# Splitting eight weight chunks on GpSimd and summing four constant rows on VectorE in a two-layer fusion kernel

## The reference, cut to what matters

```python
h = tokenise(x)                      # 16 images, 37 tokens each, width 256
h = concat([h, txt], axis=1)         # 165 tokens per batch item
h = h + scan_attention(layernorm(h))
# layer 0 FFN: 8 experts in 4 groups, each token uses one group (2 experts)
gate = silu(einsum('td,edf->tef', xf, gate_w)); up = einsum('td,edf->tef', xf, up_w)
h = h + einsum('te,tef,efd->td', w, gate * up, down_w)
h = h + rope_attention(layernorm(h))
# layer 1 FFN: 4 experts, top 2
c     = gelu(b1) @ w2 + b2           # one row of 256 per expert
c_sum = c.sum(axis=0)
out   = gates . (y_sel - c_sel + c_sum)
```

## Time and profile before

| | us |
|---|---|
| median of 3 runs | 774.32 (773.2 to 774.41) |
| the profiled execution, its own time | 773.09 |
| its span in the profile | 771.3 |
| TensorE busy | 709.3 (92%) |
| VectorE / ScalarE / GpSimd busy | 453.9 / 370.8 / 292.4 |

### The profile page before, as it was taken

The page is one execution under the profiler, slowest core; times in us unless marked ns, Lnnn a source line. Parts: engine busy times, 40 slices in busy tenths (PEclk is TensorE's granted clock), DMA queues, the critical chain, the costliest instruction groups (busy, mean ns, idle before and its releaser), DMA issues.

```text
span 771.3 us, 18144 instructions
## 1 busy us (share of the span) xinstructions
PE 709.3 (92%) x6029; PEld 619.9 (80%) x6030; DVE 453.9 (59%) x1225; ACT 370.8 (48%) x871; POOL 292.4 (38%) x259
## 2 busy tenths in 40 slices
PE   5989974999999999988899998799999999999981
PEld 5769964889888897667789986688888888888871
DVE  5897677344444443437798988745454555455540
ACT  5898744433344433333667655343434343344430
POOL 2348101222333224114445430235556655564431
PEclk9999996999999999999999999899999999999996
DMA  9897998114122112127741279112233232323235
GB/s 265 190 212 86 140 163 267 42 29 120 28 41 41 27 22 35 22 61 199 152 56 18 39 92 303 47 36 43 43 53 55 42 47 48 55 45 45 36 36 155
DMA packets 42214, 66.22 MB, mean 86 GB/s; under 512 B 3680, under 2 KB 29264, under 8 KB 41616
## 3 DMA queue, kind: packets, MB, share of 16 engines
q0 software_dynamic: 22304, 39.19, 33.2%
q1 hardware_dynamic: 19664, 25.93, 10.6%
q10 hardware_dynamic: 192, 0.38, 0.1%
HBM read 65.80 MB, written 23.35 MB: 116 GB/s over the span
## 4 chain that ended last, share of the span: by engine, by line
PE 72%; DVE 15%; ACT 4%; DMA 4%; issue 2%; POOL 1%; POOLq 0%; SPq 0%; DVEq 0%
PE PS L1145 16%; PE PS L1158 15%; PE PS L852 14%; PE PS L889 8%; PE PS L867 3%; PE PS L2455 3%; PE PS L1513 2%; PE PS L2469 2%; ACT Y L2175 2%; PE PS L1130 1%; PE PS L1540 1%; DMA xs<-Y 1%; DMA X<-in_w_dram 1%; POOL X L1767 1%; DMA ccols<-in_cols_dram 1%
## 5 line engine op out<-in xcount | busy, mean ns | idle before, releaser
L1158 PE MATMUL PS<-X 128*128 x720 | 125.8, 273 | 1.9 <-ACT X L1227 1.9
L1324 POOL DMA_INDIRECT sum<-X,dest x45 | 89.4, 1986 | 96.3 <-ACT X L1227 79.3
L1145 PE MATMUL PS<-X 128*128 128x256 f16 (+1 forms) x768 | 122.7, 265 | 0.6 <-issue 0.6
L1217 ACT ACTIVATE X<-PS,X 128x256 f32<-128x256 f32 (+1 forms) x192 | 72.8, 462 | 103.2 <-PE PS L1145 103.2
L852 PE MATMUL PS<-Y,X 128*128 128x256 f16 x960 | 108.1, 273 | 0.5 <-DVE Y L1021 0.5
L852 PEld LDWEIGHTS PS<-Y,X 128*128 x960 | 93.8, 98 | 11.5 <-issue 0.7
L1145 PE MATMUL PS<-X,Y 128*128 128x256 f16 (+1 forms) x384 | 100.2, 264 | 0.0
L1158 PE MATMUL PS<-Y,X 128*128 x360 | 98.2, 273 | 0.0
L1116 POOL DMA_INDIRECT sum<-Y,dest x24 | 38.1, 1588 | 111.9 <-DVE Y L1049 108.3
L1145 PEld LDWEIGHTS PS<-X 128*128 x768 | 71.8, 97 | 10.3 <-issue 1.1
L1158 PEld LDWEIGHTS PS<-X 128*128 128x128 f16 x720 | 70.4, 98 | 10.8 <-issue 2.9
(11 more groups left out here) (408 smaller groups left out, 1390.2 us busy)
## 6 DMA issues: line engine op xcount, KB each, us to landing
X<-in_w_dram POOLq DMA_DIRECT2D x10, 1024.0 KB, 16.1
X<-in_w_dram POOLq DMA_DIRECT2D x8, 768.0 KB, 16.6
sum<-h SPq DMA_DIRECT2D x2, 2048.0 KB, 16.2
Y<-in_w_dram POOLq DMA_DIRECT2D x4, 1024.0 KB, 11.8
xs<-Y SPq DMA_DIRECT2D x2, 1040.0 KB, 6.5
xs<-Y SPq DMA_DIRECT2D x2, 1032.0 KB, 10.4
h<-in_txt_dram SPq DMA_DIRECT2D x2, 1024.0 KB, 16.9
Y<-in_patches_dram SPq DMA_DIRECT2D x3, 672.0 KB, 7.8
```

The costliest lines, as they stand in the source:

```text
L1145: ins = nc.tensor.matmul(PS[:, 2 * s + c // 2, (c % 2) * T1:(c % 2) * T1 + tokens], part[:, off:off + P], x_[:, slot, k, 0:tokens], start= ...
L1158: ins = nc.tensor.matmul(PS[:, 4 + a, 0:D], h_[:, s, c, a * P:(a + 1) * P], part[:, off:off + D], start=(s == 0 and c == 0 and n == 0), st ...
L1217: ins = nc.scalar.activation(hh1[:, s, c, 0:tokens], PS[:, 2 * s + c // 2, (c % 2) * T1:(c % 2) * T1 + tokens], ACT.Gelu, bias=bias1[:, sl ...
L1324: nc.gpsimd.indirect_dma_start(out=sum1, out_offset=bass.IndirectOffsetOnAxis(ap=dest[:, i:i + 1], axis=0), in_=y1buf[:, u % 2, i - first_ ...
```

## The change

In layer 0 the chunks 0 to 7 are no longer transferred with a cast and an addition. SyncE loads each as f32 into one of two buffers (`stage`, 128 x 1024 f32 each), the first two at once behind its other first loads, chunk n once chunk n - 2 is split. GpSimd copies a chunk to its high half as f16 and subtracts that from the buffer into the low half. The transfers carry the other 16 chunks: four casts and four additions of four chunks. The first addition is issued behind the split of chunk 6, the other three behind that of chunk 7. ScalarE negates 16 chunks in place of 18.

In layer 1 `biases_sum` is gone with its 96 matmuls. ScalarE copies `csum`, now the sum of the `b2` rows alone, and `rest1` ahead of `act_rows`. VectorE sums the four rows and `csum` with three additions and then subtracts, ahead of `dve_experts1`; the subtraction L1290 is gone from the first unit. TensorE waits for `rows_known` before `keep_clock(85, 3)`, and has three new fillers: `keep_clock(40, 3)` behind `pe_slots`, `keep_clock(45, 3)` ahead of the experts, and `keep_clock(18, 3)` where `meanwhile` stood.

```diff
-W0C, CAST, ADDED = XW0 // CW, 4, 3
-BY_ACT = range(6, W0C)
-NEGATED = (0, 2, 2, 2, 2, 2, 2, 2, 2, 2, 0)
+W0C, CAST, ADDED = XW0 // CW, 4, 4
+BY_ACT = range(8, W0C)
+NEGATED = (0, 2, 2, 2, 2, 2, 2, 2, 2, 0, 0)
...
-            pe.wait_ge(w0_added, 16 * W0C // ADDED)
+            pe.wait_ge(own_split, BY_ACT[0])
+            pe.wait_ge(w0_added, 16 * len(BY_ACT) // ADDED)
...
                 if known(i, 0):
                     transpose_x(0, 0, 0)
-                    meanwhile()
+                    keep_clock(18, 3)
...
                 if known(i, 0):
                     split_x(0, 0)
-                    act.wait_ge(c_psum, 3)
-                    nc.scalar.activation(csum, PS[:, 6, 0:D], ACT.Copy).then_inc(c_copied, 1)
...
-            act_rows(act, 1, inrow1)
-            act.wait_ge(c_psum, 2)
+            act.wait_ge(c_psum, 3)
+            nc.scalar.activation(csum, PS[:, 6, 0:D], ACT.Copy)
             nc.scalar.activation(rest1[:, 0:2, :].rearrange("p e n -> p (e n)"), PS[:, C_BANKS[0], :], ACT.Copy)
...
+            act_rows(act, 1, inrow1)
...
             pe_count(pe, 1)
-            biases_sum(0, True, False)
-            biases_sum(1, False, False)
             biases_rest()
+            pe.wait_ge(rows_known, 2)
             keep_clock(85, 3)
             pe_slots(pe, 1, TOPK * NT, SLOT1, inrow1, intile1)
-            biases_sum(2, False, False)
+            keep_clock(40, 3)
             pe.wait_ge(slots_ready, 2)
             pe.wait_ge(dest_ready, 2)
             pe_scale(pe, 1)
             pe.wait_ge(c_copied, 1)
-            def meanwhile():
-                biases_sum(3, False, True).then_inc(c_psum, 1)
-            pe_experts1(pe, meanwhile)
+            keep_clock(45, 3)
+            pe_experts1(pe)
...
+            def rest_of_outputs():
+                dve.wait_ge(c_copied, 1)
+                pairs_, whole = y1buf[:, 0], y1buf[:, 1, 0, :]
+                chain.link(nc.vector.tensor_tensor(pairs_, rest1[:, 0:2, :], rest1[:, 2:4, :], ALU.add))
+                chain.link(nc.vector.tensor_tensor(whole, pairs_[:, 0, :], pairs_[:, 1, :], ALU.add))
+                chain.link(nc.vector.tensor_tensor(whole, whole, csum, ALU.add))
+                chain.link(nc.vector.tensor_tensor(rest1[:, :, :], whole.unsqueeze(1).broadcast_to([P, E1, D]), rest1[:, :, :],
+                                                   ALU.subtract))
+            rest_of_outputs()
             dve_experts1(dve, chain)
...
+            for n in range(BY_ACT[0]):
+                if n >= 2:
+                    sp.wait_ge(own_split, n - 1)
+                sp.dma_start(stage[:, n % 2, :], w0[:, n * CW:(n + 1) * CW]).then_inc(own_loaded[n % 2], 16)
...
             pool.wait_ge(xni_ready, IT)
             for n in range(BY_ACT[0]):
-                pool.wait_ge(w0_cast[n // CAST], 16)
-                nc.gpsimd.tensor_scalar(w0_low(n), w0_high(n), -1.0, None, ALU.mult).then_inc(own_negated, 1)
-                if n % ADDED == ADDED - 1:
-                    add(n + 1 - ADDED)
-            for first in range(BY_ACT[0], W0C, ADDED):
+                pool.wait_ge(own_loaded[n % 2], 16 * (n // 2 + 1))
+                nc.gpsimd.tensor_copy(w0_high(n), stage[:, n % 2, :]).then_inc(own_high, 1)
+                pool.wait_ge(own_high, n + 1)
+                nc.gpsimd.tensor_tensor(w0_low(n), stage[:, n % 2, :], w0_high(n), ALU.subtract).then_inc(own_split, 1)
+                if n == BY_ACT[0] - 2:
+                    add(BY_ACT[0])
+            for first in range(BY_ACT[0] + ADDED, W0C, ADDED):
                 add(first)
```

More of the change, by code:

```diff
@@ L373, in w0_source, with w0_rounded @@
             return w0[:, first * CW:(first + n) * CW].rearrange("p (c n) -> p c n", n=CW)
+        def w0_rounded(n):
+            return (own_high, n + 1) if n < BY_ACT[0] else (w0_cast[(n - BY_ACT[0]) // CAST], 16)
         def in_w0(off):
@@ L396, in build @@
         d_moved = sem("d_moved")
-        w0_cast = [sem(f"w0_cast{i}") for i in range(W0C // CAST)]
-        own_negated = sem("own_negated")
+        w0_cast = [sem(f"w0_cast{i}") for i in range(len(BY_ACT) // CAST)]
+        own_loaded = [sem(f"own_loaded{i}") for i in range(2)]
+        own_high = sem("own_high")
+        own_split = sem("own_split")
         w0_negated = sem("w0_negated")
@@ L501, in build @@
         small1_loaded = sem("small1_loaded")
-        rest_ready = sem("rest_ready")
         c_copied = sem("c_copied")
@@ L778, in pe_gram @@
                 for u in range(2):
-                    pe.wait_ge(w0_cast[(3 * e + u) // CAST], 16)
+                    pe.wait_ge(*w0_rounded(3 * e + u))
                     for n in range(KC * F0 // P):
@@ L1119, in pool_slots0, with pe_experts1 @@
             pool_slots(pool, SLOT0, 6, gather, send)
-        def pe_experts1(pe, meanwhile):
+        def pe_experts1(pe):
             def transpose_x(i, slot, j):
@@ L1287, in tile @@
                     split_x(i + 1, 1 - slot, j + slot, expert_of(i + 1))
[L1288 to L1293, removed]
                 split_h(i, 0)
@@ L1998, in pe_layer1 @@
             pe.wait_ge(small1_loaded, 16)
[L2000 to L2008, removed]
             def biases_rest():
@@ L2013, in biases_rest @@
                 for e in range(E1):
-                    nc.tensor.matmul(PS[:, 6, 0:D], onesf[0:1, :], b2all[0:1, e, :], start=False, stop=False)
+                    ins = nc.tensor.matmul(PS[:, 6, 0:D], onesf[0:1, :], b2all[0:1, e, :], start=(e == 0), stop=(e == E1 - 1))
+                ins.then_inc(c_psum, 1)
             bias_out(pe, 0, range(F1 // P // 2, F1 // P))
@@ L2135, in cast @@
             def cast(g):
-                nc.gpsimd.dma_start(w0_part(CAST * g, CAST, 0), w0_source(CAST * g, CAST)).then_inc(w0_cast[g], 16)
+                first = BY_ACT[0] + CAST * g
+                nc.gpsimd.dma_start(w0_part(first, CAST, 0), w0_source(first, CAST)).then_inc(w0_cast[g], 16)
             def add(first):
[L2141 to L2144, removed]
+                pool.wait_ge(w0_negated, first + ADDED - BY_ACT[0])
                 nc.gpsimd.dma_start(w0_part(first, ADDED, 1), w0_source(first, ADDED), accum_op=ALU.add).then_inc(w0_added, 16)
-            for g in range(W0C // CAST):
-                if g == (XW - BATCH * D) // CW // CAST:
+            for g in range(len(BY_ACT) // CAST):
+                if BY_ACT[0] + CAST * g == (XW - BATCH * D) // CW:
                     pool.wait_ge(text_tr, BATCH // 2)
@@ L2282, in negate @@
             def negate(n):
-                act.wait_ge(w0_cast[n // CAST], 16)
+                act.wait_ge(*w0_rounded(n))
                 nc.scalar.activation(w0_low(n), w0_high(n), ACT.Copy, scale=-1.0).then_inc(w0_negated, 1)
```

## The result

The changed kernel is slower. Its median over 12 runs is 777.5 us (775.42 to 778.92) beside 775.29 us (773.2 to 776.56) for 12 runs of the kernel before on the same chip: a ratio of 1.0029, with a 95% interval of 1.0019 to 1.0040, so 2.2 us more, where 2.3 us less was forecast. It lies outside the range given. The profiled execution took 778.24 us with a span of 776.4, against 773.09 and 771.3. These two executions lie 5.1 us apart, more than the medians, chiefly because the profiled execution of before is faster than any of its 12 runs.

The account below looks back on a forecast made before the run. TensorE was taken to hold 72% of the chain, so only places where the chain leaves it could change. Layer 1's -2.8 and layer 0's +0.5 gave -2.3 us: 772.0 from the median 774.32, range 769.8 to 776.5.

Parts of the forecast that it names:

- Layer 1: Start of layer 1's experts: without `meanwhile` the products wait for the split alone, 501.2 instead of 504.00, gain 2.8 us.
- Rival 2: Start of layer 1's experts: low clock returns as TensorE idles, layer 1 gives 1.1 us, total 773.7; chance 0.12.
- Layer 0, the transfers: Layer 0's DMA queues: 9.4 us less work, first addition issued at 80.3, rows land 0.45 us later, cost +0.5 us.
- The cost of one microsecond for each: Layer 0's row store: landing unchanged if the first addition is issued at 79.85; each microsecond later costs one.
- never idle until the last row lands: Layer 0's DMA engines: claimed busy without a break, so the landing moves by the difference in start less 9.4 us.
- The cap of 1.23 us: Start of layer 0's experts: even with an instant store the gather waits for source until 130.93, against 132.16.
- Rival 1: Layer 0: slow GpSimd splits, first addition at 91.5, stores land late, layer 0 costs 11.7 us, total 783.2; chance 0.18.
- a rule weighed against the trace: VectorE beside GpSimd, layer 0: skill says two-SBUF-input operations and GpSimd exclude each other; trace read as at most 0.6 us on VectorE.
- rival 3: Layer 0's attention: GpSimd's subtractions hold VectorE's scan and products, TensorE moves by 1.6 us, total up to 773.1; chance 0.10.
- +0.5: Layer 0's whole term in the forecast sum, from the rows landing 0.45 us later; -1.2 at the low end, capped by source.

Follow-up runs that it names:

- layer 0 alone: Layer 0 as in the changed kernel, layer 1 as in the kernel before: 779.19 us, ratio 1.0078 to the kernel before.
- with fillers: Changed kernel plus 60 filler matmuls on TensorE between the first output product and the scan's sum: 774.28 us, ratio 1.0012 to the kernel before.
- with four chunks: Changed kernel, but GpSimd splits only chunks 0 to 3 and 20 go by transfer: 772.76 us, ratio 0.9994 to the kernel before.
- the two halves run alone: Two kernels, each with only one layer changed against the kernel before: layer 1 770.77 us, ratio 0.9961; layer 0 779.19 us, ratio 1.0078.
- 16 fillers: Changed kernel with only two chunks split by GpSimd, plus 16 filler matmuls in TensorE's wait: 770.69 us, ratio 0.9963 to the kernel before.

## Why the prediction was wrong

**Layer 1: right.** Forecast -2.8 us, measured -3.0 alone and -2.5 in the profiled pair. The difference is small change: the gather took 3.11 us instead of 2.79. Rival 2 (the low clock returns) did not come: half clock would have made the products 4.3 us long.

**Layer 0, the transfers: the issue right, the landing not put to the test.** The first addition was forecast for 80.3 us and issued at 80.43. Two terms were off and cancelled: a chunk takes 1.04 + 2.12 us, not 1.2 + 2.4, and the seven chunks with their gaps and stalls came to 30.2 us in all, of which 22.1 are operations, so that 8 are gaps, waits and holding where 5 had been allowed. The cost of one microsecond for each that the additions are late was borne out at 82.57, at 69.46 and, to 1.2 or 1.3 us, at 87.38 and 73.00. In the kernel after itself the output loop, and with it the last rows, came too late for this to matter: the DMA engines ran empty ahead of them, against the prediction's "never idle until the last row lands". The cap of 1.23 us for this place was reached, but by luck: source was so late that the store no longer counted. By the prediction's own arithmetic an undisturbed loop would have seen the rows land at 131.88 + (80.43 - 79.85) = 132.46, 0.6 us later than before. Rival 1 did not happen.

**Layer 0, the hold: the step that failed.** It is the one called a rule weighed against the trace: "at most 0.6 us of waiting is seen on VectorE's side", and from that rival 3 with a chance of 0.10 and at most 1.6 us. Three things were wrong in it.

First, the row didn't bear what was put on it. The 2.21 us of the scan in the earlier trace rows were read as a scan held by nothing in the presence of GpSimd. The instruction beside it was this one:

```profile
63.60 2.76 POOL L2154 TENSOR_SCALAR X<-X 128x1024 f16<-128x1024 f16 x1
```

The scan began 1.76 us into it, when the 0.9 us in which a negation holds VectorE were over. The row showed a lucky moment, not that GpSimd leaves VectorE alone. The 0.6 us in the products behind it were the 0.9 us of the next negation, cut short. The subtraction that the change adds holds for 2.0 us: the scan's 3.55 us came back in the kernels after, with layer 0 alone, with fillers and with four chunks, each time with a subtraction in flight. For the subtraction the Trainium skill (SBUF — State Buffer, "Who interferes with whom") was right: the second to issue fully blocks, as 66.50 to 70.05 against 67.98 shows. For the negation the traces agree with it only over the first 0.9 us: the scan of 64.58 took 2.37 us beside one that ran until 66.61.

Second, the price was that of one collision. Since each side then waits for the other, the holds come one after the other: L2636, L2642, the scan and both products were late by 0.7, 1.7, 1.3 and 1.9 us, 5.8 us in sum with 0.1 at the start, of which VectorE's waits for ScalarE and TensorE took up 1.4 and the slack ahead of the group sums 0.5. There 3.9 us were left where 1.6 had been the most.

Third, what the idle TensorE does to its clock was asked only of layer 1, in rival 2, where the earlier trace rows showed it. In layer 0 it cost 4.57 us in the profiled execution, more than the hold, and 3.35 with layer 0 alone. With fillers and the same start of the group sums it cost 1.74, so idleness is the cause of some 1.6 to 2.8 us of it; for the remaining 1.7 that is only argued, and with one trace of each kernel the sizes are rough.

With these two terms, and with -1.2 for the wait that the late source hides in place of +0.5, the sum is 772.0 + 3.9 + 4.6 - 1.2 - 0.5 = 778.8, 4.5 above the kernel before; the profiled pair has 5.1, the medians 2.2, and the two halves run alone 3.0.

**What stays open.** Why a scan that had started first lost 0.95 us beside the issue of a transfer, and then stood behind the negation as well, when an operation in the kernel before lost nothing beside the same pair; what else moves TensorE's clock; and how much of the 8.5 us a usual execution of the kernel after loses, since only one of them was profiled, and the clock's part was 4.57 us in it and 3.35 with layer 0 alone.

## What to carry to other kernels

Before work is moved to GpSimd, list the VectorE operations with two SBUF operands that will run beside it, and give each up to one hold of GpSimd as a delay (here 0.9 us for a copy or negation of 1024 elements a partition, 2.0 for a subtraction). If they end in front of a tight wait of TensorE, add what TensorE loses at the low clock after the idleness. A row that shows no holding counts only for the same operation and the same distance between the two starts. If the work can't be moved away, instructions with a short hold on GpSimd and fillers in TensorE's wait are what to try; here neither did better than leaving layer 0 as it was.

## What the runs showed of the hardware that was not expected

- A GpSimd instruction does not hold VectorE for as long as it runs: the f16 negation for the first 0.9 of 2.76 us, the f32 to f16 copy for 0.9 of 1.04, the subtraction for 2.0 of 2.12.
- The issue of a transfer by GpSimd (65.00 to 66.26) and an f16 negation behind it held VectorE's scan to 4.05 us, in both traces with this order; with the issue moved away it took 2.37.
- A GpSimd subtraction (f32 minus f16 into f16, 128 x 1024) takes 2.12 us and the f32 to f16 copy 1.04, both faster than the f16 negation of the same shape (2.76 us).
- In one trace each, 1.10 us of idleness ahead of the group sums was followed by one group at the 1.2 GHz level (3.56 us instead of 2.03), 3.67 us by three groups at it, and 1.14 us behind 16 fillers by none.
